# Second attention: row maxima as 65-row products of one head instead of pairs of 64-row products

## The reference, cut to what matters

```python
x = x + conv_attention(gn(x), ...)       # 12 heads of 16, with relative positions
t = to_tokens(x)                         # (8, 1024, 192)
t = t + _L1_attn_ref(_ln_t(t), ...)      # the second attention, below
t = t + _L1_ffn_ref(_ln_t(t), ...)       # 16 experts, one per token

def _L1_attn_ref(hidden_states, Wq, bq, Wk, bk, Wv, bv):   # 12 heads of 16
    q, k, v = heads(h @ Wq + bq), heads(h @ Wk + bk), heads(h @ Wv + bv)
    scores = jnp.einsum('bhqd,bhkd->bhqk', q, k) / NORM    # (8, 12, 1024, 1024)
    probs = jax.nn.softmax(scores, axis=-1)
    return jnp.einsum('bhqk,bhkd->bhqd', probs, v)...
```

## Time and profile before

| | |
|---|---|
| median of three runs | 3465.89 us |
| profiled execution, its time and span | 3465.52 us, 3463.9 us |
| second attention, first maximum to last product | about 1824 to 2918 us |
| its blocks with maxima | 365: 22 steps of 16 and 13 of step 22 |
| TensorE, VectorE, ScalarE busy over the whole span | 85%, 71%, 53% |
| mean granted clock of TensorE | 0.89 |

### The profile page before, as it was taken

One profiled execution on the slowest core, in us unless ns is written; L12 is line 12 of the kernel. 1 busy time (PEld: TensorE's weight loads), 2 busy tenths in 40 slices (PEclk: granted clock), 3 DMA queues, 4 the chain that ended last, 5 costly groups with the idle time before them and its releaser, 6 DMA issues. The chain is left out here.

```text
span 3463.9 us, 64326 instructions
## 1 busy us (share of the span) xinstructions
PE 2933.3 (85%) x17814; PEld 1149.3 (33%) x17815; DVE 2453.6 (71%) x4484; ACT 1853.0 (53%) x2382; POOL 1034.8 (30%) x1685
## 2 busy tenths in 40 slices
PE   4886799999999999969969999999999996432777
PEld 2764122222222222226641222222222221431666
DVE  3553799899998998915438999999999993341221
ACT  2433166666666666654422777777777775110332
POOL 0000333333333333213313333323323320233665
PEclk9766599999999999988986999999999998555877
DMA  4666555454444554425653222222222223920211
GB/s 85 204 200 196 111 103 102 102 107 100 99 102 96 102 106 103 87 72 154 173 152 55 67 66 67 64 65 68 66 67 66 66 58 87 161 59 8 57 50 34
DMA packets 292226, 327.79 MB, mean 95 GB/s; under 512 B 137404, under 2 KB 224262, under 8 KB 287522
## 3 DMA queue, kind: packets, MB, share of 16 engines
q0 software_dynamic: 76576, 192.17, 24.5%
q1 hardware_dynamic: 182340, 121.85, 13.5%
q10 hardware_dynamic: 33216, 12.58, 2.2%
HBM read 217.71 MB, written 109.19 MB: 94 GB/s over the span
## 5 line engine op out<-in xcount | busy, mean ns | idle before, releaser
L494 DVE TENSOR_REDUCE a_halfmax<-a_psR 128x1 f32<-128x512 f32 x3072 | 1964.1, 686 | 190.0 <-PE a_psR L345 171.9
L449 ACT ACTIVATE a_probs<-a_psS 128x1024 f32<-128x1024 f32 x1536 | 1488.4, 1021 | 791.9 <-PE a_psS L363 787.4
L363 PE MATMUL a_psS<-a_qrows,a_krows 121*128 121x512 f16 (+1 forms) x3072 | 806.8, 384 | 55.2 <-DMA a_qrows<-relh 50.8
L374 PE MATMUL a_psO<-a_probs,a_v 128*32 128x512 f32 x6144 | 826.4, 610 | 1.2 <-ACT a_probs L449 1.2
L345 PE MATMUL a_psR<-a_kmax,a_qmax 64*128 64x512 f16 x3072 | 685.2, 400 | 78.5 <-DMA a_qmax<-relh 42.2
L345 PEld LDWEIGHTS a_psR<-a_kmax,a_qmax 64*128 64x128 f16 x3072 | 161.1, 93 | 1068.7 <-DVE a_halfmax L494 948.9
L363 PEld LDWEIGHTS a_psS<-a_qrows,a_krows 121*128 121x128 f16 (+1 forms) x3072 | 242.9, 98 | 429.0 <-issue 162.1
L204 POOL DMA_DIRECT2D a_qmax<-qk x240 | 122.4, 510 | 667.8 <-PE a_psO L374 603.4
L188 POOL DMA_DIRECT2D a_qrows<-qk x240 | 123.6, 515 | 276.6 <-PE a_psO L374 257.2
L825 PE MATMUL p_psQ<-p_xnT,p_wqk 96*128 96x512 f32 x384 | 187.0, 650 | 20.4 <-DVE p_xnT L982 13.9
L374 PEld LDWEIGHTS a_psO<-a_probs,a_v 128*32 128x32 f32 x6144 | 121.4, 108 | 184.3 <-issue 176.4
(11 more groups left out here) (163 smaller groups left out, 2391.6 us busy)
## 6 DMA issues: line engine op xcount, KB each, us to landing
a_qrows<-qk POOLq DMA_DIRECT2D x240, 128.0 KB, 3.7
qk<-p_half SPq DMA_DIRECT2D x96, 256.0 KB, 3.4
v<-p_v SPq DMA_DIRECT2D x48, 512.0 KB, 6.1
a_qrows<-rel POOLq DMA_DIRECT2D x96, 256.0 KB, 4.5
a_v<-v POOLq DMA_DIRECT2D x96, 256.0 KB, 3.1
a_krows<-qk POOLq DMA_DIRECT2D x168, 128.0 KB, 3.8
a_qmax<-qk POOLq DMA_DIRECT2D x288, 64.0 KB, 2.3
a_kmax<-qk POOLq DMA_DIRECT2D x240, 64.0 KB, 2.3
```

What stands on the lines that cost most here:

```text
L363: mm = nc.tensor.matmul(psS[:, (2 * n + j) % 4, :], K[buf][:, h, keys], A[buf][kt % NA][:, h, queries], start=True, stop=True)
L374: mm = nc.tensor.matmul(psO[32 * h:32 * h + 32, :], V[buf][:, kt, h, :], PT[:, blk % 2, h, :], start=(kt == 0), stop=(kt == KT - 1))
L449: nc.scalar.activation(PT[:, blk % 2, 2 * pair:2 * pair + 2, :], psS[:, b0:b0 + 2, :], ACT.Exp, scale=scale).then_inc(exped, 1)
L494: nc.vector.tensor_reduce(mx[:, unit, half:half + 1], psR[:, slot, :], AX.X, ALU.max)\
```

## The change

The operands of the second attention's maximum products get the layout of the score products: 65 partitions, all four heads side by side in the free dimension. Row 64 of both is filled once with zeros (row `REL + 1` of `onehot_dram`), so that a maximum product has 65 rows instead of 64 and stands alone in the array, as a score product does. The head of a job is `2 * r + p`. The values, the number of maximum products, their 512 columns and their order are as before. The loads become 8 DMAs of 128 KB a step instead of 16 of 64 KB, in blocks 0, 2, 4 and 6. SyncE issues four small DMAs more for row 64 at the start, and TensorE waits for them once. The first attention keeps its form.

```diff
--- before.py
+++ after.py
@@ -69,8 +69,8 @@
         else:
             A = [[sb(f"qrows{i}", [KR, GH, L], F16)] for i in range(2)]
             K = [sb(f"krows{i}", [KR, GH, L], F16) for i in range(2)]
-            AM = [[sb(f"qmax{i}", [P, 2, L], F16)] * 2 for i in range(2)]
-            KM = [sb(f"kmax{i}", [P, 2, L], F16) for i in range(2)]
+            AM = [sb(f"qmax{i}", [KR, GH, L], F16) for i in range(2)]
+            KM = [sb(f"kmax{i}", [KR, GH, L], F16) for i in range(2)]
         V = [sb(f"v{i}", [P, KT, GH, VW], F32) for i in range(2)]
         PT = sb("probs", [P, 2, GH, 512], F32)
         MX = [sb(f"halfmax{i}", [P, UNITS, 2], F32) for i in range(2)]
@@ -104,7 +104,7 @@
 
         TERMS = ((0, 0), (0, 1), (1, 0)) if rel else ((0, 0), (0, 1), (1, 0), (1, 1))
         NLOAD = ((NA + 1) * 3 + NA * 3 + 2) if rel else 2 * 4 + 2
-        NLOADM = 2 * (2 + 2 + 3) if rel else 2 * 2 * 4
+        NLOADM = 2 * (2 + 2 + 3) if rel else 2 * 4
         NROW = NA
         CONSTS = 16 * 2 * (11 if rel else 1)
         NREL = 6
@@ -199,10 +199,15 @@
                 x = slice(KT // 2 * part, KT // 2 * part + KT // 2)
                 pool.dma_start(V[buf][:, x, :, :], VN[s][:, x, :, :]).then_inc(loaded[buf], 16)
 
-            def load_max_terms(s, buf, r, n):
-                of = slice(64 * r + HD * n, 64 * r + HD * n + HD)
-                pool.dma_start(AM[buf][0][of, :, :], qk_pair(s, TERMS[n][0], 0, r)).then_inc(loadedm[buf], 16)
-                pool.dma_start(KM[buf][of, :, :], qk_pair(s, TERMS[n][1], 1, r)).then_inc(loadedm[buf], 16)
+            def load_max_terms(s, buf, x):
+                if rel:
+                    of = slice(64 * x, 64 * x + HD)
+                    pool.dma_start(AM[buf][0][of, :, :], qk_pair(s, 0, 0, x)).then_inc(loadedm[buf], 16)
+                    pool.dma_start(KM[buf][of, :, :], qk_pair(s, 0, 1, x)).then_inc(loadedm[buf], 16)
+                else:
+                    of = slice(HD * x, HD * x + HD)
+                    pool.dma_start(AM[buf][of, :, :], qk(s, TERMS[x][0], 0)).then_inc(loadedm[buf], 16)
+                    pool.dma_start(KM[buf][of, :, :], qk(s, TERMS[x][1], 1)).then_inc(loadedm[buf], 16)
 
             def load_max_rel(s, buf, r, half):
                 am, at = AM[buf][half], 64 * r
@@ -218,12 +223,12 @@
 
                 if rel:
                     if blk == 0:
-                        load_max_terms(s, buf, 0, 0)
-                        load_max_terms(s, buf, 1, 0)
+                        load_max_terms(s, buf, 0)
+                        load_max_terms(s, buf, 1)
                     elif blk < 5:
                         load_max_rel(s, buf, blk % 2, (blk - 1) // 2)
-                elif blk < 8:
-                    load_max_terms(s, buf, blk % 2, blk // 2)
+                elif blk % 2 == 0 and blk < 8:
+                    load_max_terms(s, buf, blk // 2)
 
             def load(s, buf, blk):
 
@@ -296,6 +301,9 @@
                         cols = slice(512 * half, 512 * half + 512)
                         sp.dma_start(KM[i][at + WI:64 * r + 64, :, cols],
                                      every(onehot_dram[16 * half:16 * half + 16, cols], 2)).then_inc(const_km[i], 16)
+            for i in range(0 if rel else 2):
+                for t in (AM[i], KM[i]):
+                    sp.dma_start(t[R:KR, :, :], every(onehot_dram[REL + 1:REL + 2, :], GH)).then_inc(const_km[i], 16)
             sp.wait_ge(loadedm[0], 16 * NLOADM)
             for i in range(2):
                 if rel:
@@ -341,9 +349,12 @@
                 if j[0] == "max":
                     r, half, p, qt, _ = max_of(j[1])
                     b = (buf + j[2]) % 2
-                    at = slice(64 * r, 64 * r + MR)
-                    mm = nc.tensor.matmul(psR[:, slot, :], AM[b][half][at, p, P * qt:P * qt + P],
-                                          KM[b][at, p, 512 * half:512 * half + 512], start=True, stop=True)
+                    if rel:
+                        at, am, x = slice(64 * r, 64 * r + MR), AM[b][half], p
+                    else:
+                        at, am, x = slice(0, KR), AM[b], 2 * r + p
+                    mm = nc.tensor.matmul(psR[:, slot, :], am[at, x, P * qt:P * qt + P],
+                                          KM[b][at, x, 512 * half:512 * half + 512], start=True, stop=True)
                 elif j[0] == "rows":
                     pe.wait_ge(maxed, rows + 1)
                     mm = nc.tensor.transpose(psR[0:UNITS, slot, 0:P], MC[:, :], ident[:, :])
@@ -409,14 +420,12 @@
                         job(jn, j, base, slot(jn), free(jn), u, halves, s + 1)
 
             pe.wait_ge(const_done, 2)
-            if rel:
-                pe.wait_ge(const_km[0], 16 * 6)
+            pe.wait_ge(const_km[0], 16 * (6 if rel else 2))
             pe.wait_ge(loadedm[0], 16 * NLOADM)
             for n, j in enumerate(FIRST):
                 if n == HALVES + 1:
                     pe.wait_ge(loadedm[1], 16 * NLOADM)
-                    if rel:
-                        pe.wait_ge(const_km[1], 16 * 6)
+                    pe.wait_ge(const_km[1], 16 * (6 if rel else 2))
                 job(n, j, 0, first_slot(n), n + 1, 0, 0, 0)
             pe.wait_ge(const_dma, CONSTS)
             for u in range(2):
```

## The result

The changed kernel took 3584.93 us as the median of four runs (3553.43 to 3648.23), the kernel before 3464.28 us (3458.03 to 3470.01). The ratio is 1.032, with an interval of 1.0259 to 1.0381; ratios in this document leave out a run that is over 1.5% above the fastest of its kernel, here that of 3648.23 us. The forecast was 3525 us, 3511 to 3547: the direction was right, the size was not. The four runs lie 95 us apart where those of before lie 12 apart, and the slower a run, the lower its mean granted clock: 3553.43 us at 0.883, 3569.89 at 0.876, 3599.98 at 0.872, 3648.23 at 0.857. The profiled run is the fastest of the four, with a span of 3551.5 us, 87.6 more than before.

What follows compares the result with a forecast made beforehand. TensorE was taken to bound the second attention. From the profiled 3465.5 us, +79 for the maximum products, -6 - 8 - 5 for waits, +1 for the cold stretch and -2 for the loads gave 3525 us, range 3511 to 3547.

Steps and rivals of the forecast that it cites:

- TensorE sets the pace of the steady part: Second attention's steady blocks: TensorE has no hole in its 2.61 us, VectorE alone could do its maxima in 2.41.
- A pair costs 0.432 instead of 0.325: Two maximum products in sequence, without the change of form from scores: +0.107 us a pair, +79 us in all.
- Waits that go: Places where TensorE stands still for VectorE should close as VectorE gets 0.42 us of slack a block: -19 us.
- back jobs: Transposes there start 0.46 us after the last pair, which costs 0.32; 45 such waits for VectorE go: -6 us.
- rows jobs: The pair behind one takes 0.76 us instead of 0.39, its second product waiting for a bank; 22 such waits go: -8.
- loop ends: End of the two-step loop: late scores and a drawn-out first pair, some 0.45 us in 10 iterations, go: -5 us.
- The loads: Before the first maximum of the second attention: 8 load issues instead of 16, each load landing later; -2 us.
- The cold stretch: Some 6 pairs at the 1.2 GHz level cost +0.31 us each instead of +0.107: +1 us beyond the sum.
- The new form does not flow: Rival, chance 0.05: going between scores and maxima still costs a change of form, two a block, +73 us: 3598 us.
- TensorE keeps its waits: Rival, chance 0.12: back, rows and loop jobs cost what they cost, something other than VectorE holding them: 3545 us.
- VectorE sets the pace: Rival, chance 0.06: added columns fall into TensorE's waits ahead of each pair, block stays at 2.61 us: 3464 us.

Runs made afterwards that it cites:

- rows64_single: The changed kernel with its second-attention maximum products cut to rows 0 to 63, row 64 left out; one run, 3687.89 us.
- warm_after: The changed kernel with three small 128-row identity products ahead of each of the prologue's last 26 maximum products; ratio 1.0189 to the kernel before.

## Why the prediction was wrong

- *TensorE sets the pace of the steady part; VectorE's waits are apparent.* Right. The block grew by the 0.22 us that the columns ask for, and VectorE took up idle time.
- *A pair costs 0.432 instead of 0.325; two of four changes of form go, at 0.10 each.* Right, and shown from the other side by rows64_single.
- *Waits that go, -19 us.* Right as a sum: 58.2 us were measured where 351 blocks alone make 76 to 77. By the starts of the blocks in both traces, one with a back job takes 3.23 us before and 3.27 after (0.62 and 0.44 above a plain one), one with a rows job 3.19 and 2.99 (0.58 and 0.16), a loop end costs 0.47 and 0.27 us. So the 44 back jobs gave 8 us (forecast 6), the 21 rows jobs 9 (8), the loop ends 2 (5): the loop's end was priced too high, and the other two made up for it.
- *The loads, -2 us.* Wrong in sign, and small. From GpSimd's first instruction in the stage to the first maximum 11.4 us passed before and 12.6 after (1812.50 to 1823.94, 1809.83 to 1822.45). That the first maximum still came 1.5 us earlier in the span is due to the stages ahead. In the versions without the four row DMAs it was 11.9 to 12.1, so these have some part in it. The larger part lies, as far as the traces tell, in the landing time: the sum took 3.7 us for a 128 KB load, the median of another load over the whole kernel, but between 1808 and 1823 us, where these loads are in flight together, the medians were 7.2 us (`a_qmax`) and 7.8 (`a_kmax`).
- *The cold stretch, +1 us, with -5 to +3 as its bounds.* This is the step that failed. It took the stretch's length as given, six pairs, and priced only what stands in it. Its thoughts on the length were that denser work might raise the clock sooner, or that the stretch might grow in step with its blocks. The price of a cold block was right (5.39 us instead of 4.77), the number of them was not: 74 us instead of 14 in the best run, so that the term measured +28 us (31.1 less 14 x 0.217) where the sum had +1. The rest of the distance from that run to the median stays open. The trace of before held a sign that was not read: the row of the stretch shows TensorE busy 13.64 of 14.00 us at clock 0.51, so busy time alone didn't raise it even there.
- *The rivals.* None had this mechanism. "The new form does not flow" (3598 us) came nearest to the median and "TensorE keeps its waits" (3545 us) to the profiled run, both by luck: the rows refute the first by the block of 2.83 us, the second by the waits that went. "VectorE sets the pace" is refuted by the same block.

The forecast's ratio was 3525/3465.5 = 1.017, and the changed kernel whose maxima span 128 rows, with a cold stretch of 10 us, measured 1.0179 (1.0155 to 1.0203). That bears out the other terms of the sum, though the unchanged stage behind alone can move such a ratio by a few tenths of a per cent.

## What to carry to other kernels

When a change makes matmuls use fewer rows of the array at once, look at every place where the clock is low and ask whether it will still rise there; a stream without gaps at half clock looks fully busy. Unused rows of an operand can be filled with zeros at no cost in array time, and here the low level then ended early, in both layouts. And where two engines are both near 100%, compare the pace of the same instruction where its engine runs alone with its pace in the stage: this told the bound where the table of waits named the wrong engine.

## What the runs showed of the hardware

Two things had not been expected. At equal columns and order, the time that TensorE stayed at 1.2 GHz after the steps began went with how many rows its products had: 244 us with single 64-row maxima (one profile), 74 us with 65 (two profiles), 10 to 13 us with 96 or 128 rows for one of the two kinds of product (three), 3 us with 128 for both (one); and 14 us with pairs of 64-row products side by side, 3 with 128-row scores beside them (one each). Once at 2.4 GHz, the same 65-row stream held it for 1000 us. The Trainium skill, "TensorE: Matmul & The Clock Gate", Part 1, describes the warm-up as a matter of sustained time at work. The traces agree for the 128-row fillers of warm_after, where the clock rose 5.7 us after the first, and differ for the 65-row stream, which was busy for 74 us before it rose; the measurement decides. Why runs of the changed kernel differ so much in time and mean clock stays open. The other is the price of a change between a 64-row and a 65-row product: 0.10 us at 2.4 GHz, each way (0.97 us from four scores to the maxima and 0.53 back in rows64_single, where 0.865 and 0.432 are columns), with a difference of a single row.
